# Three query buffers, deviations ahead of the output's low parts, and identity products in five waits of a decoder kernel

## The reference

```
x = ln(x + conv(x));  x = ln(x + xattn(x, ctx));  x = ln(x + lowrank_ffn(x))      # layer 0
x = ln(x + retention(x));  x = ln(x + xattn(x, ctx, mask));  x = ln(x + gated_ffn(x))   # layer 1

retention:  q, k = rope(x Wq), rope(x Wk);  v = x Wv           # 16 heads of 32
            out = ((q k^T / sqrt(32)) * decay) v               # 100 x 100 per batch and head
            out = (out - mean) * rsqrt(var + eps)              # per token and head
            return (out * gn_weight + gn_bias) Wo
```

## Time and profile before

| | |
|---|---|
| median of 3 runs | 2209.33 us (2198.43, 2209.99, 2209.33) |
| the profiled execution: its time, its span | 2207.1 us, 2205.3 us |
| PE busy, instructions | 2080.2 us (94%), 12700 |
| DVE, ACT, POOL busy | 46%, 43%, 36% |
| mean granted TensorE clock | 0.986 |

### The profile page before, as it was taken

The page is one execution under the profiler, slowest core; times in us unless marked ns, Lnnn a source line. Parts: engine busy times, 40 slices in busy tenths (PEclk is TensorE's granted clock), DMA queues, the critical chain, the costliest instruction groups (busy, mean ns, idle before and its releaser), DMA issues.

```text
span 2205.3 us, 36789 instructions
## 1 busy us (share of the span) xinstructions
PE 2080.2 (94%) x12700; PEld 1921.8 (87%) x12700; DVE 1020.0 (46%) x1685; ACT 951.6 (43%) x1663; POOL 785.3 (36%) x635
## 2 busy tenths in 40 slices
PE   4899999999889999899999999899999999999997
PEld 4788888888778778788888888899999999999987
DVE  8566666666673576466566666556100003000032
ACT  2356565556662444455565655422222223111141
POOL 0434333234456345323443332322232232222244
PEclk9999999999999899999999999999999999999999
DMA  5465555446321212754655554212111112111123
GB/s 174 132 166 154 151 137 156 135 136 162 109 67 29 80 30 86 217 141 131 163 153 155 137 154 121 69 58 66 58 57 64 60 57 64 60 57 62 61 76 97
DMA packets 140378, 233.86 MB, mean 106 GB/s; under 512 B 49240, under 2 KB 93528, under 8 KB 140184
## 3 DMA queue, kind: packets, MB, share of 16 engines
q1 hardware_dynamic: 140312, 232.99, 36.9%
HBM read 174.12 MB, written 55.53 MB: 104 GB/s over the span
## 4 chain that ended last, share of the span: by engine, by line
PE 77%; DVE 8%; ACT 5%; issue 3%; POOL 3%; DMA 3%; SPq 1%; DVEq 0%; POOLq 0%; ACTq 0%
PE psS L345 14%; PE psS L347 14%; PE psS L346 14%; PE psO L1925 5%; PE psJ L345 4%; PE psJ L346 3%; PE psJ L347 3%; PE psS L1884 3%; PE psT L1911 2%; PE psT L345 2%; PE psT L347 2%; PE psT L346 2%; PE psS L1911 2%; PE psO L346 1%; PE psO L345 1%
## 5 line engine op out<-in xcount | busy, mean ns | idle before, releaser
L797 POOL TENSOR_TENSOR fw_lo<-raw,fw_hi 128x1024 fp32r<-128x1024 f32 x96 | 236.3, 2461 | 543.2 <-ACT fw_hi L1108 543.2
L345 PE MATMUL psS<-hid_hi,fw_hi 128*128 128x400 f32 x1152 | 396.8, 344 | 3.5 <-DVE hid_lo L1807 2.9
L347 PE MATMUL psS<-hid_hi,fw_lo 128*128 128x400 f32 x1152 | 397.8, 345 | 0.0
L346 PE MATMUL psS<-hid_lo,fw_hi 128*128 128x400 f32 x1152 | 397.4, 345 | 0.0
L589 POOL TENSOR_TENSOR pT<-p,pT 128x600 fp32r<-128x600 f32 x128 | 188.8, 1475 | 531.6 <-ACT pT L896 530.2
L1335 DVE TENSOR_REDUCE psS<-psS 100x1 f32<-100x722 f32 x256 | 234.7, 917 | 153.7 <-PE psS L1884 153.3
L1807 DVE TENSOR_TENSOR hid_lo<-h_act,hid_hi 128x800 fp32r<-128x800 f32 x32 | 38.5, 1272 | 530.3 <-ACT hid_hi L1231 530.3
L345 PEld LDWEIGHTS psS<-hid_hi,fw_hi 128*128 128x128 f32 x1152 | 216.2, 188 | 7.4 <-DVE hid_lo L1807 5.1
L347 PEld LDWEIGHTS psS<-hid_hi,fw_lo 128*128 128x128 f32 x1152 | 217.5, 189 | 0.0
L346 PEld LDWEIGHTS psS<-hid_lo,fw_hi 128*128 128x128 f32 x1152 | 216.1, 188 | 0.0
L345 PE MATMUL psJ<-cT_hi,wk_hi 128*128 128x362 f32 (+1 forms) x512 | 181.4, 354 | 36.3 <-DVE cT_lo L1329 15.6
(11 more groups left out here) (347 smaller groups left out, 4448.7 us busy)
## 6 DMA issues: line engine op xcount, KB each, us to landing
kS<-k_parts SPq DMA_DIRECT2D x384, 180.5 KB
raw<-ffn_dram SPq DMA_DIRECT2D x96, 512.0 KB, 3.6
k_parts<-kst SPq DMA_DIRECT2D x64, 362.0 KB, 3.4
k_parts<-kst SPq DMA_DIRECT2D x64, 360.0 KB, 3.0
ctx_raw<-ctxT_dram SPq DMA_DIRECT2D x32, 361.0 KB, 4.0
qS<-q_parts SPq DMA_DIRECT2D x192, 50.0 KB, 2.6
q_parts<-qst SPq DMA_DIRECT2D x16, 400.0 KB, 2.5
ctx_late<-ctxT_dram SPq DMA_DIRECT2D x14, 362.0 KB, 5.0
```

What stands on the lines that cost most here:

```text
L345: nc.tensor.matmul(out, st[0], mv_[0], start=first, stop=False)
L346: nc.tensor.matmul(out, st[0], mv_[1], start=False, stop=False)
L347: return nc.tensor.matmul(out, st[1], mv_[0], start=False, stop=last)
L797: nc.gpsimd.tensor_tensor(fw.lo[:, e, :], raw[:, e, :], fw.hi[:, e, :], ALU.subtract)\
```

## The change

Three things change. In retention, the three instructions of the deviations are put into a function, and where another batch follows, they stand ahead of `retention_output_lo` on DVE instead of behind it. The last batch keeps its order. The outgoing queries get a third buffer, `qst_third`, and a third semaphore, so that `query_hi` waits for the sending of unit u-3; and SP sends the fifth unit (unit 4) ahead of the first `queries_in`. And `keep_running` is called at five more places of PE's queue, 36 products in all.

```diff
+        top[0] = craw_at
+        qst_third = at("qst_third", [P, 2, HALF], f32r)
...
+        def query_buffer(u):
+            return qst_third if u % 3 == 2 else qst[:, u % 3]
+
+        def query_outs(L, n):
+
+            return tuple((q_outs[r], 16 * (3 * L + sum(u % 3 == r for u in range(n)) - (L if r == 2 else 0)))
+                         for r in range(3))
...
                         queries_out(L, range(C))
-                    sp.wait_ge(A.q_out0, 16 * C * L + 32)
-                    sp.wait_ge(A.q_out1, 16 * C * L + 32)
+                    queries_out(L, (C,))
+                    for s, n in query_outs(L, C):
+                        sp.wait_ge(s, n)
                     queries_in(L, 0, 0)
-                    queries_out(L, range(C, 2 * C))
+                    queries_out(L, range(C + 1, 2 * C))
...
-                if u >= 2:
-                    act.wait_ge((A.q_out0, A.q_out1)[u % 2], 16 * (n // 2))
-                dst, src = qst[:, u % 2, 0, :], q_bank[u % 2][:, 0:HALF]
+                if u >= 3:
+                    act.wait_ge(*query_outs(L, u - 2)[u % 3])
+                dst, src = query_buffer(u)[:, 0, :], q_bank[u % 2][:, 0:HALF]
...
+                if after:
+                    deviations(b)
                 if prev:
                     retention_output_lo(b)
                 if not after:
                     for c in range(C):
                         context_lo(1, c)
-                dve.wait_ge(R.pv_mm, C * b + C)
...
+                    deviations(b)
                 if after:
                     retention_values_lo(b + 1)
...
             pe.wait_ge(w_split, BLOCKS["v1"])
+            keep_running(psJ, 9)
             ffn0_in(0)
...
             for u in range(2 * M + 2):
+                if u == 2:
+                    keep_running(psJ, 5)
...
                 if u == 2:
+                    keep_running(psJ, 4)
                     pe.wait_ge(w_split, BLOCKS["u2"] + 1)
...
+            keep_running(psT, 10)
             pe.wait_ge(w_split, BLOCKS["rk"] + 2)
...
                 if prev:
                     retention_output(b)
+                else:
+                    keep_running(psJ, 8)
```

More of the change, by code:

```diff
@@ L127, in decoder_kernel @@
         next_at = top[0]
+        top[0] = craw_at
+        qst_third = at("qst_third", [P, 2, HALF], f32r)
+        assert top[0] <= next_at
         top[0] = craw_at
@@ L288, in decoder_kernel @@
         A = sems("att_", "ctx_in0 ctx_in1 more_in late_a late_b ctx_hi ctx_even ctx_odd half_hi half_lo k_mm k_hi k_lo kd_out0 kd_out1 ks_in0 ks_in1 ks_in2 ks_in3 v_mm v_hi v_lo "
-                         "q_mm q_hi q_lo q_out0 q_out1 qs_in0 qs_in1 qs_in2 qs_in3 s_mm maxed nm_hi nm t_mm rows_set st_mm exped pt_hi lo_even lo_odd pv_mm "
+                         "q_mm q_hi q_lo q_out0 q_out1 q_out2 qs_in0 qs_in1 qs_in2 qs_in3 s_mm maxed nm_hi nm t_mm rows_set st_mm exped pt_hi lo_even lo_odd pv_mm "
                          "u_done sums r_done z_done x_done o_sum o_scaled o_biased o_hi o_lo resid_done mask_in mask_done shift "
@@ L297, in decoder_kernel @@
         rows_in, apart = sem("rows_in"), sem("apart")
+        q_outs = (A.q_out0, A.q_out1, A.q_out2)
         def wait(eng, s, v):
@@ L415, in queries_out @@
                     sp.dma_start(q_dram[:, :, m, h * HALF:(h + 1) * HALF].rearrange("x p t -> p x t"),
-                                 qst[:, u % 2, :, :].bitcast(fp32)).then_inc((A.q_out0, A.q_out1)[u % 2], 16)
+                                 query_buffer(u)[:, :, :].bitcast(fp32)).then_inc(q_outs[u % 3], 16)
             def queries_in(L, b, g):
@@ L480, in first @@
                     queries_in(L, 0, 3)
-                    sp.wait_ge(A.q_out0, 16 * C * (L + 1))
-                    sp.wait_ge(A.q_out1, 16 * C * (L + 1))
+                    for s, n in query_outs(L, 2 * C):
+                        sp.wait_ge(s, n)
                     keys_out(L, 0, 2, 0)
@@ L1311, in query_lo @@
                 dve.wait_ge(A.q_hi, 2 * C * L + u + 1)
-                hi, lo, src = qst[:, u % 2, 0, :], qst[:, u % 2, 1, :], q_bank[u % 2][:, 0:HALF]
+                hi, lo, src = query_buffer(u)[:, 0, :], query_buffer(u)[:, 1, :], q_bank[u % 2][:, 0:HALF]
                 if L == 0:
@@ L1669, in group_norm, with deviations @@
                   .then_inc(R.g_norm, 1)
+            def deviations(b):
+                dve.wait_ge(R.pv_mm, C * b + C)
+                nc.vector.tensor_reduce(gsum[:, :], heads(psO[0:T, 0:D]), AX.X, ALU.add).then_inc(R.g_sum, 1)
+                dve.wait_ge(R.g_sum, b + 1)
+                nc.vector.tensor_scalar(gneg[:, :], gsum[:, :], -1.0 / HD, None, ALU.mult).then_inc(R.g_mean, 1)
+                dve.wait_ge(R.g_mean, b + 1)
+                nc.vector.tensor_tensor(heads(gd[:, :]), heads(psO[0:T, 0:D]), spread(gneg), ALU.add)\
+                  .then_inc(R.g_dev, 1)
             def retention_output_lo(b):
```

## The result

The changed kernel takes 2192.85 us (median of 4 runs, 2190.80 to 2195.86), the kernel before 2209.66 (4 runs, 2198.43 to 2210.22): a ratio of 0.9931, interval 0.9903 to 0.9958. The forecast was 2188.5, −0.9%; it came out as −0.7%. The profiled execution has a span of 2189.0 us, 16.3 less than before, where the sum was 18.6.

What follows compares the result with a forecast made beforehand. PE, busy 94% of the span, bounds the kernel, by waits or lowered clock. Terms 13.2 + 1.2 + 1.3 + 1.0 + 1.9 = 18.6 us off the profiled 2207.1 give 2188.5 (chance 0.70), range 2181 to 2200.

Steps and rivals of the forecast that it cites:

- Retention, 13.2: Six retention batches gain 13.2 us: 3.9 from waits, the other nine from half clock; bounds 0 and 13.7.
- the eight products: Identity products in the 2.06 us wait ahead of retention's batch 1, to keep the clock up at 745; share within 13.2.
- the batch at 775.16: Retention batch of 13.44 us before the change: waits 0.88, then reaches the next at full speed; taken as evidence for the gain.
- Low-rank FFN, 1.2: Products in PE's waits there keep ten later products from half clock: gain 1.2 us, from 0 to 1.6.
- Retention's first queries, 1.3: Ten products fill the 3.1 us wait for the decay's DMA; nine behind run at full clock: gain 1.3, 0 to 1.4.
- Layer 0's queries, 1.0: The third query buffer removes PE's 0.97 us wait at 81.82: gain 1.0, from 0 to 1.0.
- My bound of 0: Layer 0's queries gain nothing if the turn of ACT and DVE sets the pace anyway.
- Layer 1's queries, 1.9: Waiting for the earlier-sent unit 4 cuts PE's 2.84 us wait to about 0.9: gain 1.9, bounds 0 and 2.84.
- Rival 1: Clock still falls in retention, which gains only its waits, 3.9: 2197.8, or 2200.3 if falls elsewhere stay; chance 0.13.
- Rival 2: In retention `gsq` issues ahead of `r_oT_lo`, PE waits 1.1 us a batch; with clock falls 18.69 a batch, 2225; chance 0.03.
- Rival 3: The last four terms, outside retention's batches, are absorbed by other waits; only 13.2 counts: 2193.9; chance 0.10.
- Rival 4: The 36 identity products, 8.5 us, overrun their waits: 2197, with some at half clock 2200; chance 0.04.

Runs made afterwards that it cites:

- run 1: The kernel before with only the deviations moved ahead of the output's low part: 2202.38 us, ratio 0.9972 to the kernel before.
- run 4: The changed kernel without the eight identity products ahead of retention's batch 1: 2194.61 us, ratio 0.9941 to the kernel before.
- run 2: The kernel before with only the 36 identity products added: 2201.75 us, ratio 0.9972 to the kernel before.
- run 3: The kernel before with only the third query buffer and the early sending of unit 4: 2207.80 us, ratio 0.9997 to the kernel before.
- run 6: The changed kernel without the move of the deviations, buffers and products kept: 2201.77 us, ratio 0.9979 to the kernel before.
- run 8: The changed kernel as it is, timed and profiled again: 2191.95 us, ratio 0.9931 to the kernel before.
- run 5: The changed kernel with the next values' low part ahead of `r_oT_lo` on DVE: 2195.17 us, ratio 0.9949 to the kernel before.
- run 9: The changed kernel with the next values' low part and two unread reductions ahead of `r_oT_lo` on DVE: 2211.91 us, ratio 1.0010 to the kernel before.

## Why the prediction was right, step by step

**Retention, 13.2:** 13.04 between the two profiled executions, and by its own steps: a period of 12.56 for 12.55, no wait for `pb_lo`, `r_oT_lo` in its usual 0.57. The split into waits and clock was near: over all executions the clock gives about 12 us to the whole change, where the text had nine here and 2.5 in the next two terms. (Its 4.5 for the waits holds batch 0's 0.54, which stayed; in the six batches they were 4.0.) What was wrong is who brings the clock's share. The text had the eight products keep the clock up at 745; run 1's profile held it without them, and by run 4 they are worth some 2 us. The waits of 0.89 that I called harmless, by the batch at 775.16, are not always so: of the fifteen of 0.88 and 0.89 in the profiles of the kernel before and of runs 2, 3 and 6, two had a long fall 1.2 to 1.4 us behind them. Putting them back (run 6) costs 9.8 us in the median; 4.6 are their own length, and where the rest arises is not shown. And 13 is the gain over one execution. Alone, the move brings 0.28% (run 1), some 6 us, mostly waits.

**Low-rank FFN, 1.2:** 0.78. The ten half-clock products are gone, but PE runs into later waits for `f_g_lo`. Nine products in the first wait cost nothing, as said: 0.56 us of it are left. At the end of the stage the ten products ahead of retention's first query cost a little. PE came to them late, partly at half clock, and in the chain that ended last they stand directly ahead of that query:

```profile
663.94 2.60 PE psT L1868 x20
```

From the issue of the decay's DMA to the query it is 7.70 us, against 7.53 before and 7.07 in run 8, where PE still waits: 0.2 to 0.6 us too long.

**Retention's first queries, 1.3:** 1.32.

**Layer 0's queries, 1.0:** PE's wait went, and 0.7 of it were left behind the waits for key loads, with 5 us more at half clock in between; in run 3, with as much half clock as before, 0.9. In run 8, where PE waited 1.97 for keys and the clock fell behind that, none was. My bound of 0 came from ACT's and DVE's turn; what can take the gain back is half clock and the chain of key loads. That 0.07 is all that shows at the low-rank FFN comes of the 0.58 lost ahead of the queries, which the sum did not provide for.

**Layer 1's queries, 1.9:** 1.80 at the keys, with PE's wait at 1.16 for "about 0.9". Behind it waits for the mask and key loads take back what the clock gave there:

```profile
PE psS L1902 <- DMA kS<-mask_bias: 2.4, 3, 1.6
```

0.7 us of these were there before, in two waits. In the timing of run 3 the two buffer terms together can be told neither from 0 nor from their 2.9.

**Rivals.** Rival 1 (clock still falls): no fall in retention in either profile of the changed kernel. Rival 2: shown wrong by run 5, and its period of 18.69 was far over run 5's 13.22. The Trainium skill's rule that it drew on ("SBUF — State Buffer", "Who interferes with whom": whichever issues first holds the pair) agrees with the earlier trace rows for `x_res` and differs from run 5's `r_oT_lo`, the VectorE instruction issued second, which was not held; the measurement decides. Rival 3: wrong for all four terms in the first profile, though in run 8's layer 0's came to nothing; and the measured median, 2192.85, lies nearer to its 2193.9 than to the forecast's 2188.5, and the timings of the small terms cannot rule it out. Rival 4: of the 36 products only the ten clearly ended behind their wait.

**The sum:** 18.6 against 16.3; the missing 2.3 are the 0.58 ahead of layer 0's queries, 0.3 in them, the FFN's 0.4, 0.6 behind the last step and smaller ones.

## What to carry to other kernels

Where the busiest engine's clock can fall, price a short wait at more than its length, but as a chance that differs from execution to execution: one profile shows one draw, so read several before putting a figure on it. Fill such waits only where what follows is bound by the engine itself, since ahead of a chain of transfers part of the time won is waited away, and only where the engine does wait. When two instructions are released by different things, let the one that is ready earlier go first: here three instructions used 0.9 of the 1.79 us that DVE stood idle in each batch.

## What the runs showed of the hardware that was not expected

Waits of 0.66 us in each batch left the clock at 1.00 for 79 us (run 5); of six waits of 1.80 to 1.96 us three had a stretch at half clock behind them, 3.4 us each (run 9); one wait of 2.06 us had none in run 1, 3.4 us in run 4 and over 13 us in the kernel before and in run 3; and two waits of 0.89 us had 6.8 and 17 us behind them, thirteen others of 0.88 and 0.89 none. A VectorE subtraction of 0.57 us kept its time beside a GpSimd square that started 0.39 us ahead of it, and the square went from 1.04 to 1.85 us; another subtraction of the same run went from 0.57 to 1.85.
